# Recurrent stage: time stored in four groups by remainder, the root of beta folded into key and value, the gate moved between units, and another order ahead of them

## The reference, cut to what matters

```python
xn = x * rsqrt(mean(x * x, -1) + 1e-6) * rms_w
proj = xn @ in_proj_W.T + in_proj_b              # z, K (two parts), V
u = silu(causal_conv4(V) + conv_b)               # four taps over time, per channel
...                                              # heads of u: alpha, omega, sel_B, sel_C, beta, gates
omega = omega + arange(s) * rope
Kh = K * sel_B
Vg = u * (vp * u_gate)
Q = (u @ Q_W.T) * sel_C
def step(Sc, inp):                               # scanned over the 1024 steps
    Sr = stack([a11 * S0 + a12 * S1, -a12 * S0 + a11 * S1])
    err = v - sum(k * Sr)
    Sn = Sr + bt * err * k
y = sum(Q * Y, -1)
y = groupnorm(y) * gn_w + gn_b; y = y * silu(z); y = y + D * u
return residual + y @ out_W.T
```

## Time and profile before

| | us |
|---|---|
| median of 3 runs (3330.17 to 3335.16) | 3331.11 |
| the profiled execution, its own time | 3331.97 |
| its span, first to last instruction | 3330.1 |
| of it the recurrent stage, from its first instruction at 1205 to the last addition at 2012 | about 807 |
| busy share over the span: PE, DVE, ACT, POOL | 79%, 60%, 28%, 13% |

### The profile page before, as it was taken

The page is one execution under the profiler, slowest core; times in us unless marked ns, Lnnn a source line. Parts: engine busy times, 40 slices in busy tenths (PEclk is TensorE's granted clock), DMA queues, the critical chain, the costliest instruction groups (busy, mean ns, idle before and its releaser), DMA issues. The chain is left out here.

```text
span 3330.1 us, 38590 instructions
## 1 busy us (share of the span) xinstructions
PE 2624.0 (79%) x12216; PEld 1704.3 (51%) x12216; DVE 1986.9 (60%) x3875; ACT 945.7 (28%) x1701; POOL 446.3 (13%) x304
## 2 busy tenths in 40 slices
PE   5888988779999685566565545698889866999998
PEld 2454544368888453333223322355444435878887
DVE  3765666244543265999989984666656433555554
ACT  1344434222222133011211112144334412222222
POOL 0000000044320210211001110000000012112110
PEclk8899989889999897887777777799999977999999
DMA  1000000021100110000000000000000001001000
GB/s 61 17 9 22 17 9 1 7 102 51 52 23 0 54 56 7 7 7 7 13 7 7 0 0 30 34 9 30 10 9 9 1 8 64 32 32 63 31 31 25
DMA packets 19327, 79.41 MB, mean 24 GB/s; under 512 B 4696, under 2 KB 5720, under 8 KB 15192
## 3 DMA queue, kind: packets, MB, share of 16 engines
q1 hardware_dynamic: 19168, 77.36, 6.6%
HBM read 70.99 MB, written 2.16 MB: 22 GB/s over the span
## 5 line engine op out<-in xcount | busy, mean ns | idle before, releaser
L617 DVE CUSTOM_DVE_ANT_0 a_junk<-pair,a_mask 128x512 f32<-128x512 f32 (+3 forms) x768 | 393.4, 555 | 239.9 <-PE pair L461 226.3
L554 ACT ACTIVATE a_prob<-pair 128x512 f32<-128x512 f32 (+3 forms) x768 | 362.2, 490 | 418.5 <-PE pair L484 407.0
L484 PE MATMUL pair<-a_qx,a_kx 128*128 128x512 f32 (+3 forms) x768 | 332.6, 447 | 34.5 <-issue 20.4
L461 PE MATMUL pair<-a_kx,a_qx 128*128 128x512 f32 (+3 forms) x768 | 283.1, 420 | 52.4 <-DVE a_mx_raw L617 44.6
L439 PE MATMUL pair<-a_hc,a_w 128*128 128x512 f32 x512 | 262.1, 638 | 72.0 <-DMA a_w<-in_L_qkv 59.3
L484 PEld LDWEIGHTS pair<-a_qx,a_kx 128*128 128x128 f32 x768 | 146.5, 196 | 208.4 <-issue 132.9
L907 DVE TENSOR_TENSOR mx_h<-pair,mx_g 128x512 f32<-128x512 f32 x128 | 88.5, 692 | 267.9 <-PE pair L726 258.4
L461 PEld LDWEIGHTS pair<-a_kx,a_qx 128*128 128x128 f32 x768 | 150.6, 201 | 152.0 <-DVE a_mx_raw L617 124.5
L414 POOL TENSOR_SCALAR_AFFINE_SELECT a_prob<-a_prob 128x512 f32<-128x512 f32 x128 | 81.3, 636 | 1078.6 <-ACT a_prob L554 1078.6
L724 PE MATMUL pair<-mx_x_hi,mx_w_lo 128*128 128x512 f32 x512 | 201.8, 394 | 24.4 <-POOL mx_w_lo L788 21.8
L724 PE MATMUL pair<-m_x_hi,m_w_lo 128*128 128x512 f32 x448 | 177.3, 396 | 48.8 <-POOL m_w_lo L788 46.8
(11 more groups left out here) (246 smaller groups left out, 4926.4 us busy)
## 6 DMA issues: line engine op xcount, KB each, us to landing
m_raw<-in_L_cond_experts SPq DMA_DIRECT2D x18, 1024.0 KB, 4.8
mx_raw<-in_L_ffn_experts SPq DMA_DIRECT2D x24, 512.0 KB, 5.2
a_w<-in_L_qkv SPq DMA_DIRECT2D x16, 640.0 KB, 3.8
mx_wt<-expert_weights SPq DMA_DIRECT2D x8, 1024.0 KB, 4.7
a_hc<-h_stream SPq DMA_DIRECT2D x8, 512.0 KB, 3.3
r_w_ring<-in_r_q_w SPq DMA_DIRECT2D x8, 512.0 KB, 3.6
m_raw<-in_L_cond_experts SPq DMA_DIRECT2D x6, 512.0 KB, 3.4
x_stream<-in_x SPq DMA_DIRECT2D x1, 2048.0 KB, 7.3
```

What stands on the lines that cost most here:

```text
L461: nc.tensor.matmul(first_bank[t % FR][:, 0:c1 - c0], qx[:, next_buf, a, i * P:(i + 1) * P], kx[:, next_buf, a // 2, c0:c1], start=True, st ...
L484: nc.tensor.matmul(score_bank[t % SR][:, q0:TT], kx[:, buf, a // 2, j * P:(j + 1) * P], qx[:, buf, a, h * TT + q0:(h + 1) * TT], start=Tru ...
L554: nc.scalar.activation(prob[:, i % RING, a, q0:TT], score_bank[(i * GH + a) % SR][:, q0:TT], ACT.Exp, scale=SCALE).then_inc(s["b_exp"], 1)
L617: nc.vector.tensor_tensor_reduce(out=junk[:, t % 2, 0:cols], in0=first_bank[t % FR][:, 0:cols], in1=mask[:, m0:m0 + cols], scale=1.0, scal ...
```

## The change

Time step t = 4*i + g is now stored in group g at place i (GT = 256 places a group). PE reads the normalized input with a step of four elements (`by_step`), so that V, K and z come out in the new order, and reads `ybuf` group by group (`in_order`), one element from each of four places 256 elements apart, so that the projection comes out in the old order. The tree's levels 0 and 1 combine whole groups, later levels work inside group 3. The convolution's taps become 7 instructions for a block (a shift of k steps is another group, partly shifted by one place). The key and the value are multiplied by the root of beta already as head vectors, so the step `bk` and its spread go. POOL's two rows go to `crow`, in `prods`, and `o` no longer waits for `e`. The outputs are four multiplications of 1024 elements. `gate(r-1)` stands behind `outputs(r)`, other than at unit 4. Ahead of the units, there is one `mean` tile of four 32-row quadrants, one root and one reciprocal, and four PE tiles `inv` spread the result; ACT does the first three heads, then part A of the head math, the other seven heads, part B, the key of unit 0, part C; silu of sequence 1 comes behind z of unit 0.

```diff
+TG = 4
+GT = T // TG
+PAD_T = TG * (GT + 1)
...
-SPREADS = [V_SB0, V_SB1, V_A11, V_A12, V_BETA, V_VF]
-COEF_DVE = [(0, "kh"), (0, "t"), (0, "bk"), (0, "v"), (1, "kh"), (1, "t"), (0, "e"), (0, "diag"), (0, "m01"), (0, "m10"),
-            (1, "bk"), (1, "v"), (1, "e"), (1, "diag"), (1, "m01"), (1, "m10")]
+SPREADS = [V_SB0, V_SB1, V_A11, V_A12, V_VF]
+COEF_DVE = [(h, o) for h in range(HALF_T) for o in ("kh", "v", "t")] + \
+           [(h, o) for h in range(HALF_T) for o in ("e", "diag", "m01", "m10")]
...
+        def by_step(arr, b, k, h):
+            return seq(arr, b)[:, k, :].rearrange("p (i g) -> p g i", g=TG)[:, 2 * h:2 * h + 2, :]
+
+        def in_order(arr, k, h):
+            return arr[:, k, :].rearrange("p (g i) -> p i g", g=TG)[:, h * TT // TG:(h + 1) * TT // TG, :]
...
+                            pe.wait_ge(s["sq"], B * KD)
                             for k in range(KD):
+                                for q in range(NT):
+                                    last = nc.tensor.matmul(bank[q * H:(q + 1) * H, :], c.mean_ones[:, 0:H],
...
+                        elif what == "inv":
+                            last = nc.tensor.matmul(bank, c.ident[:, q * H:q * H + 1].broadcast_to([P, P]), inverse,
...
-                            pe.wait_ge(s["xn"], (b * HALF_T + h + 1) * KD)
+                            pe.wait_ge(s["xn"], (b + 1) * HALF_T * KD)
                             for k in range(KD):
-                                last = nc.tensor.matmul(bank, w_v[:, k, m * P:(m + 1) * P], seq(c.h, b)[:, k, half(h)],
+                                last = nc.tensor.matmul(bank, w_v[:, k, m * P:(m + 1) * P], by_step(c.h, b, k, h),
...
-                                                        seq(c.h, b)[:, k, half(h)], start=k == 0, stop=k == KD - 1)
+                                                        by_step(c.h, b, k, h), start=k == 0, stop=k == KD - 1)
...
-                                last = nc.tensor.matmul(bank, w_o[:, k, o * P:(o + 1) * P], ybuf[:, k, half(h)],
+                                last = nc.tensor.matmul(bank, w_o[:, k, o * P:(o + 1) * P], in_order(ybuf, k, h),
...
-                for m in range(KI):
-                    silu_u(1, m)
                 constants()
-                for i in range(len(HEADS_OUT)):
+                for i in FIRST_HEADS:
                     evict_head(0, i)
+                head_math(0, "A")
+                for i in MIDDLE_HEADS + LAST_HEADS:
+                    evict_head(0, i)
+                head_math(0, "B")
                 evict_k(0)
-                head_math(0)
+                head_math(0, "C")
                 for r in range(NU):
...
                     evict_z(r)
+                    if r == 0:
+                        for m in range(KI):
+                            silu_u(1, m)
...
-                        tt(coef[:, 2, half(h)], rows[:, 0, 0, half(h)], rows[:, 1, 1, half(h)], ALU.subtract).then_inc(s["cp"], 1)
-                        tt(coef[:, 5, half(h)], rows[:, 0, 1, half(h)], rows[:, 1, 0, half(h)], ALU.add).then_inc(s["cp"], 1)
+                        tt(crow[:, 0, half(h)], rows[:, 0, 0, half(h)], rows[:, 1, 1, half(h)], ALU.subtract).then_inc(s["cp"], 1)
+                        tt(crow[:, 1, half(h)], rows[:, 0, 1, half(h)], rows[:, 1, 0, half(h)], ALU.add).then_inc(s["cp"], 1)
                     for h in range(HALF_T):
-                        pool.wait_ge(s["cd"], d_at(r, h, "e"))
...
+                        sel = hq[:, b, V_SB0:V_SB1 + 1, :]
+                        did(tt(sel, sel, hq[:, b, V_BETA:V_BETA + 1, :].broadcast_to([P, 2, QW_]), ALU.mult))
...
+                def tree(level):
+                    w = 2 << (level - 2)
+                    return group(TG - 1).rearrange("p a (n w) -> p a n w", w=w), w, GT // w
+
                 def up(level):
...
+                    if level == 0:
+                        combine(group(0), group(1), GT)
+                        combine(group(2), group(3), GT)
+                    elif level == 1:
+                        combine(group(1), group(3), GT)
...
+                    elif level == 1:
+                        advance((group(1)[:, :, 1:GT], last[:, :, 0:GT - 1], GT - 1))
+                    elif level == 0:
+                        advance((group(0)[:, :, 1:GT], last[:, :, 0:GT - 1], GT - 1), (group(2), group(1), GT))
...
-                    if r:
+                    if r == KI:
                         gate(r - 1)
...
-                            for j in range(2):
-                                if x:
-                                    dve.wait_ge(s["d1"], (r * HALF_T + h) * 4 + j + 1)
-                                tt(coef[:, 2 + 3 * j, half(h)], coef[:, 2 + 3 * j, half(h)], query_banks(h)[2 * x + j], ALU.mult).then_inc(s["d1"], 1)
+                            if x:
+                                dve.wait_ge(s["d1"], r * READ + 2 * h + 1)
+                            tt(offset(h), offset(h), query_pair(h, x), ALU.mult).then_inc(s["d1"], 1)
+                    if r and r != KI:
+                        gate(r - 1)
```

More of the change, by code:

```diff
@@ L1100, in taken @@
 def taken(tile):
+    if tile[0] == "inv":
+        return "xn", (tile[1] + 1) * KD
     dve = tile[0] in BY_DVE
-    return "gd" if dve else "ga", sum((t[0] in BY_DVE) == dve for t in RING_ALL[:RING_ALL.index(tile) + 1])
+    return "gd" if dve else "ga", sum(t[0] != "inv" and (t[0] in BY_DVE) == dve for t in RING_ALL[:RING_ALL.index(tile) + 1])
 def recurrent(c, A):
@@ L1399, in dve @@
                         act.wait_ge(s["h2"], b * HEAD_DVE + n)
[L1401 to L1409, removed]
@@ L1422, in head_math @@
-                    step(T_L1, T_L2, ACT.Sqrt)
+                    t_ = lambda i: tmp[:, i, :]
+                    if part == "A":
+                        act.wait_ge(s["ga"], taken(("head", b, 1))[1])
+                        step(t_(T_E1), t_(T_AL), ACT.Abs)
+                        step(t_(T_E2), t_(T_DT), ACT.Abs)
+                        own()
+                        step(t_(T_X), t_(T_E1), ACT.Exp, scale=-1.0)
+                        step(t_(T_Y), t_(T_E2), ACT.Exp, scale=-1.0)
+                        own()
+                        step(t_(T_L1), t_(T_X), ACT.Ln, bias=1.0)
+                        step(t_(T_L2), t_(T_Y), ACT.Ln, bias=1.0)
+                        dve(1)
+                        step(t_(T_Z), t_(T_OM), ACT.Abs)
+                    elif part == "B":
+                        dve(8)
+                        step(t_(T_X), t_(T_A), ACT.Square, bias=1.0)
+                        step(t_(T_Y), t_(T_A), ACT.Square, bias=1.0, scale=-1.0)
+                        step(t_(T_Z), t_(T_W), ACT.Square)
+                        step(t_(T_E1), t_(T_A), ACT.Square)
+                    else:
+                        dve(17)
+                        step(t_(T_L1), t_(T_E2), ACT.Ln)
+                        dve(18)
+                        step(t_(T_L2), t_(T_L1), ACT.Exp)
+                        act.wait_ge(s["ga"], taken(("head", b, HEADS_OUT.index(H_BETA)))[1])
+                        step(hq[:, b, V_BETA, :], hq[:, b, V_BETA, :], ACT.Sqrt)
+                        dve(21)
+                        step(t_(T_L1), t_(T_L2), ACT.Sqrt)
@@ L1448, in _ @@
                 act.wait_ge(s["const"], 7 * 16)
-                for t in range(NT):
-                    bank = tile_in(("mean", t))
-                    nc.scalar.activation(roots[:, t * TT:(t + 1) * TT], bank, ACT.Sqrt, bias=eps[:, 0:1]).then_inc(s["ga"], 1)
+                bank = tile_in(("mean",))
+                nc.scalar.activation(roots, bank, ACT.Sqrt, bias=eps[:, 0:1]).then_inc(s["ga"], 1)
                 for m in range(KI):
@@ L1475, in _ @@
                     if r == KI - 1:
-                        head_math(1)
+                        for part in "ABC":
+                            head_math(1, part)
                 sums(NU - 1)
@@ L1580, in head_math @@
                         acts(12)
+                        dve.wait_ge(s["ga"], taken(("head", b, HEADS_OUT.index(H_RG)))[1])
                         did(tt(t_(T_L1), t_(T_L1), t_(T_R), ALU.mult))
@@ L1660, in combine, with group @@
                     own()
[L1662 to L1675 removed]
+                def group(g):
+                    return coef[:, :, g * GT:(g + 1) * GT]
@@ new lines, in advance @@
+                def advance(*moves):
+                    parts = []
+                    for x, (target, before, n) in enumerate(moves):
+                        pr = prods[:, x * 4 * GT:x * 4 * GT + 4 * n].rearrange("p (i j n) -> p i j n", i=2, j=2)
+                        mat = target.rearrange("p (i q) n -> p i q n", i=2)
+                        state = before.rearrange("p (i q) n -> p i q n", i=2)[:, :, 2, :]
+                        parts.append((pr, mat))
+                        did(tt(pr, mat[:, :, 0:2, :], state.unsqueeze(1).broadcast_to([P, 2, 2, n]), ALU.mult))
```

153 lines of the change are left out of this document (68 added, 85 removed).

## The result

The changed kernel takes 3340.68 us (median of 12 runs, 3335.03 to 3348.74), the kernel before 3333.51 beside it (12 runs, 3329.79 to 3337.66). The ratio is 1.0023, 95% interval 1.0013 to 1.0033: slightly slower, where I had predicted 3241 and a range of 3218 to 3335. The profiled execution took 3335.03 (span 3333.1). Differences are rounded after they are taken.

A forecast was written before the change was run, and what follows sets the result against it. DVE's work in the units and its waits for ACT ahead of them were taken as the bounds. Terms -54.1 - 14.8 + 2.7 + 1.1 + 1.2 - 26.2 = -90.1 gave 3241 us, range 3218 to 3335.

The forecast's parts named there:

- open term: PE's strided reads for V, K, z and projections: taken at no cost; upper bound 0.96 us an instruction instead of 0.43.
- Rival 1: PE reads at DVE's strided rate, 2.2 times as long: 111 us lost, 3352 us in all; chance 0.17.
- factor near 2: PE's strided reads take about twice as long, total 3300 to 3335 us; chance 0.10.
- What is late next: Unit 1's scan: PE's last query and the second group norm root still come in time, by 4 and 3 us.
- Tree: DVE's scan levels, up and down: levels 0 to 2 change, level 3 does not; 54.1 us saved over eight scans.
- Coefficients: DVE and POOL ahead of each scan: dropping `bk` gains almost nothing as they wait for each other; 2.7 us lost over eight.
- Gate: Six gates of 2.46 us move behind the outputs, hidden in DVE's wait for PE's spreads: 14.8 us saved.
- Ahead of the units: Chain before unit 0: one reciprocal, earlier taps and ACT's new order save 26.2 us, bounds 18 and 30.
- Rival 2: Only the projections pay for strided reads, or all of PE pays little: 34 us, about 3276; chance 0.13 (to 3300).
- rival 3: POOL and DVE do not meet as thought: 18 us either way, 3223 or 3259; within the first case's 0.55.
- rival 4: The chain ahead of the units yields only 18 us: 3249 us in all; within the first case's 0.55.

The follow-up runs named there:

- e1: The changed kernel with PE reading the normalized input and ybuf plainly (output not the reference's): 3255.46 us, ratio 0.9754 to the kernel before.
- e5: The changed kernel, but DVE writes the stage's input in four groups and PE reads it plainly: 3258.91 us, ratio 0.9765 to the kernel before.
- e6: e5 with each POOL `o` put directly behind its `c1`: 3263.80 us, ratio 0.9783 to the kernel before.
- e9: e6 with POOL's second `o` waiting for DVE's second `e`: 3241.88 us, ratio 0.9722 to the kernel before.
- e12: e5 with a multiplication of the old `bk`'s size behind each `t` (output not the reference's): 3261.61 us, ratio 0.9770 to the kernel before.
- e2: e1 with ybuf read strided again for the projections, V, K and z plain (output not the reference's): 3279.06 us, ratio 0.9822 to the kernel before.

## Why the prediction was wrong

**The step that failed** is the open term. I took PE's strided reads at no cost since PE "has reading time over" in a column of these matmuls. It has none to give: 0.90 us an instruction for 0.43, near the upper end that I had drawn from DVE (0.96). The rows pointed there: the only reads in them from 16 bytes on were DVE's at levels 1 and 2, both slow, and I let an argument without a row outweigh them. Rival 1 named the mechanism, place by place, and gave it 0.17; with 3352 it overpriced it. The line for a factor near 2, 3300 to 3335 at 0.10, had the factor right (2.09) and ended just below the measured 3341. What the loss was made of, forecast and measured: ahead of the units 39 and 35.1 (head math ends at 121.0 for 85.9), the roots 38 and 27.4, the projections 34 and 25.3. The V tile takes 3.60, not 3.85, since I gave PE the 1.88 ns an element of DVE, and it takes 1.76. For the projections I doubled plain instructions of 0.51 to 0.53, which ran at a mean granted clock of 0.82 and 0.84; the strided ones take 0.88, a factor of 1.7. Together 84.4 (the three parts come to 87.8, and some 3 are given back elsewhere) for 111. That the loss outruns the gain only above a factor of about 1.9 was nearly so: at 2.09, loss and gain are 84.4 and 81.5.

**"What is late next"** failed through this alone. In unit 1 the root was to be there 17.5 us after the scan's start and asked for at 20.6; it was asked for at 21.1 (1443.61) and there at 25.6. In `e1` it is there at 17.5 and asked for at 21.1. So the slack of 3 us was right (3.6), and the strided key tiles ate it, in six units.

**The rest of the sum held.** With plain reads the stage gains 81.2 (`e5`) to 81.5 (`e1`) where the sum says 90.1:

- Tree: 5.92 and 3.26 us for levels 1 and 2, forecast 5.93 and 3.16. Downward, levels 2, 1 and 0 take 1.64, 2.71 and 5.05 (DVE's timeline of unit 0, after), forecast 1.63, 2.70, and 5.01. Level 3, which the sum left as it was, got longer: 2.64 before and 2.84 after (unit 1), some 1.6 over eight scans.

```profile
1386.59 0.69 DVE L1717 TENSOR_TENSOR r_region<-r_region 128x508 f32<-128x508 f32 x1
...
1388.23 1.22 DVE L1717 TENSOR_TENSOR r_region<-r_region 128x1020 f32<-128x1020 f32 x1
...
1390.94 2.36 DVE L1717 TENSOR_TENSOR r_region<-r_region 128x1020 f32<-128x1020 f32 x2
...
1395.99 4.86 DVE L1790 TENSOR_TENSOR r_region<-r_region,pair 128x1024 f32<-128x1024 f32 x4
```

- Coefficients: first `e` to scan 11.63 (1340.36 to 1351.99), forecast 11.6. The mechanism (each waits for the other) is shown by `e6` and `e9`, the worth of `bk` by `e12`. What I didn't see is that the wait could be taken away: 12 us lay there.
- Gate: 10.9 for 14.8. I had named the cause as a bound, POOL's addition taking the second SBUF read, and had counted it in the last unit alone; it comes in each, at 0.65.
- Ahead of the units: 22.0 for 26.2. Taps begin 22.8 us into the stage, not 21.4; a block is 5.02, not 4.9; and from the last tap to the end of head math it is 23.0, not 21.2. The largest wait left there stands ahead of part C, on ACT (`e1`):

```profile
1284.83 0.43 DVE L1595 TENSOR_TENSOR r_tmp<-r_tmp 128x256 f32<-128x256 f32 x1 [4.84 <-ACT r_tmp L1413]
```

Gate, head chain and level 3 come to 9.7 (3.9, 4.2 and 1.6) where 8.6 to 8.9 are missing; what gave back the rest I have not traced to a row. Rival 2 is excluded by `e2` together with `e1` (V, K and z are the larger part), rival 3 by the 11.63, and rival 4 is half true: 22.0 lies midway between its 18 and my 26.2.

## What to carry to other kernels

A layout that makes one engine's reads contiguous makes another's strided: price every reader of the new layout before the one that gains, and with a strided row from any engine if the trace has no other. Put the reordering into the writer that has the least to do (here four pairs of DVE instructions, 0.6 to 0.7 us more each, and the additions that read the result back) instead of into a read that is repeated (here 320 instructions of PE). And where an engine gets faster, list what it now asks for earlier with the slack of each: here 3 us of slack turned into waits of 4.6, six times.

## What the runs showed of the hardware

- PE's fp32 matmul of 512 columns takes 0.43 us with elements 4 bytes apart, 0.45 at 8, 0.68 at 12, 0.90 at 16, 0.93 at 32 and 0.88 at 1 KB: the cost is in the moves between 16-byte pieces, and from 16 bytes on it is nearly the same for near and for far.
- A strided one hardly heeds the clock, a plain one does. Behind 14.4 us of idle time PE's first eight key instructions of unit 1 run at a mean granted clock of 0.72 (0.69 in `e1`; 1.00 is 2.4 GHz and the lower level is 1.2 GHz), the next ones at 1.00. Strided they take 0.94 and then 0.91 us each (first fence, the changed kernel), plain 0.65 and 0.45 (second, `e1`):

```profile
1422.50 7.54 PE L1267 MATMUL pair<-h_stream,r_w_kz 128*128 128x512 f32 x8 [14.42 <-DVE r_region L1668]
...
1430.02 14.62 PE L1267 MATMUL pair<-h_stream,r_w_kz 128*128 128x512 f32 x16
```

```profile
1396.08 5.23 PE L1267 MATMUL pair<-h_stream,r_w_kz 128*128 128x512 f32 x8 [14.43 <-DVE r_region L1668]
...
1401.29 5.40 PE L1267 MATMUL pair<-h_stream,r_w_kz 128*128 128x512 f32 x12
```

- A DVE instruction with two SBUF inputs and one of POOL's run one after the other, whole: 2.28 becomes 4.42. Who is first is decided by 0.07 us, and one wait that looks like a loss gave back 12 to 16 us in eight units.
